# A second buffer for the attention's broadcast target scores, filled eight source tiles before a block's end

## What is computed

```python
x = (meta_x @ W).reshape(N, HEADS, DIM)
a_src = jnp.sum(x * att_src, axis=-1)
a_dst = jnp.sum(x * att_dst, axis=-1)
logits = jax.nn.leaky_relu(a_src[src] + a_dst[dst], NEG_SLOPE)
seg_max = jax.ops.segment_max(logits, dst, num_segments=N)
ex = jnp.exp(logits - seg_max[dst])
alpha = ex / (jax.ops.segment_sum(ex, dst, num_segments=N)[dst] + 1e-16)
out = jax.ops.segment_sum(x[src] * alpha[:, :, None], dst, num_segments=N)
return out.mean(axis=1) + bias
```

## Time and profile before

| | us |
|---|---|
| median of 3 runs (1284.82 to 1287.27) | 1287.16 |
| the profiled execution | 1286.68 |
| its span | 1284.9 |
| counting edges into `C`, to about 408 | 408 |
| hops and the second and third layers, to about 826 | 418 |
| attention, 826 to 1275 | 449 |
| last norm and output | 10 |

### The profile page before, as it was taken

The page is one execution under the profiler, slowest core; times in us unless marked ns, Lnnn a source line. Parts: engine busy times, 40 slices in busy tenths (PEclk is TensorE's granted clock), DMA queues, the critical chain, the costliest instruction groups (busy, mean ns, idle before and its releaser), DMA issues.

```text
span 1284.9 us, 40100 instructions
## 1 busy us (share of the span) xinstructions
PE 1154.3 (90%) x16724; PEld 1074.0 (84%) x16724; DVE 871.6 (68%) x2375; ACT 632.7 (49%) x1161; POOL 62.8 (5%) x113
## 2 busy tenths in 40 slices
PE   0588888888999999999998899599999999999996
PEld 0588888888999999999954899488878888887996
DVE  1899999996443434344642535688878888887887
ACT  0577767661000000000112402578888788788886
POOL 2000000001111111111000002000000000000000
PEclk9866665568999999999999799599999999999998
DMA  1544444420000000000000000000000000000000
GB/s 29 83 71 62 71 61 69 70 51 11 2 3 3 3 3 2 3 3 3 3 2 1 2 3 2 2 2 2 2 2 2 2 2 2 2 2 2 7 12 13
DMA packets 133768, 21.42 MB, mean 17 GB/s; under 512 B 133041, under 2 KB 133458, under 8 KB 133618
## 3 DMA queue, kind: packets, MB, share of 16 engines
q1 hardware_dynamic: 132190, 18.75, 9.7%
q10 hardware_dynamic: 1332, 0.33, 0.1%
q0 software_dynamic: 96, 0.16, 0.0%
HBM read 18.43 MB, written 0.80 MB: 15 GB/s over the span
## 4 chain that ended last, share of the span: by engine, by line
PE 59%; DVE 25%; ACT 7%; issue 6%; DMA 1%; SPq 1%; POOL 0%; DVEq 0%; ACTq 0%; POOLq 0%
PE bank L1786 31%; PE bank L1906 11%; DVE ohk L989 6%; PE bank L1902 6%; ACT Mr L900 4%; DVE ohp L991 4%; DVE Mr L1503 3%; PE bank L1731 3%; DVE raw L979 2%; PE bank L1723 1%; DVE Mr L1510 1%; PE bank L1642 1%; PE bank L1897 1%; DVE oht L949 1%; ACT F L863 1%
## 5 line engine op out<-in xcount | busy, mean ns | idle before, releaser
L1786 PE MATMUL bank<-GH,C 128*128 128x128 f16 x7100 | 397.9, 219 | 0.0
L1786 PEld LDWEIGHTS bank<-GH,C 128*128 128x128 f16 x7100 | 396.9, 98 | 0.1
L1906 PE MATMUL bank<-F,Mr 128*128 128x260 f16 (+1 forms) x2520 | 343.9, 269 | 7.2 <-DVE Mr L1503 3.7
L900 ACT ACTIVATE Mr<-eaT 128x640 f16<-128x640 f32 x433 | 326.5, 822 | 30.0 <-PE bank L1906 28.2
L1906 PEld LDWEIGHTS bank<-F,Mr 128*128 128x128 f16 x2520 | 218.9, 98 | 30.8 <-DVE Mr L1503 4.3
L1503 DVE TENSOR_TENSOR Mr<-Mr,C 128x640 f16<-128x640 f16 x433 | 195.2, 485 | 72.9 <-ACT Mr L900 71.2
L1902 PE MATMUL bank<-FN,C 128*128 128x130 f16 x2260 | 210.0, 220 | 0.8 <-DVE r L1411 0.8
L747 ACT ACTIVATE plo<-bank 128x256 f32<-128x256 f32 (+1 forms) x84 | 30.2, 361 | 362.7 <-PE bank L1786 346.6
L1148 DVE TENSOR_TENSOR S<-bank,plo 128x256 f32<-128x256 f32 (+1 forms) x84 | 33.2, 395 | 210.7 <-ACT plo L747 210.7
L1902 PEld LDWEIGHTS bank<-FN,C 128*128 128x128 f16 x2260 | 164.2, 98 | 10.5 <-DVE r L1411 1.4
L1642 PE MATMUL bank<-ohk,ohp 128*128 128x100 f16 (+3 forms) x1452 | 159.9, 270 | 3.0 <-DVE ohp L991 3.0
(11 more groups left out here) (250 smaller groups left out, 959.6 us busy)
## 6 DMA issues: line engine op xcount, KB each, us to landing
raw<-in_edges_dram SPq DMA_DIRECT2D x242, 68.0 KB, 2.1
xs<-in_x_dram SPq DMA_DIRECT2D x1, 800.0 KB, 4.1
out_dram<-xs SPq DMA_DIRECT2D x4, 160.0 KB
wg<-in_L_gnn_W_dram ACTq DMA_DIRECT2D x2, 64.0 KB
z<-in_L_gnn_att_src_dram SPq DMA_DIRECT2D x1, 128.0 KB, 2.7
z<-in_L_gnn_att_dst_dram SPq DMA_DIRECT2D x1, 128.0 KB, 3.0
out_dram<-xs SPq DMA_DIRECT2D x1, 128.0 KB
wts<-in_L_gnn_W_dram ACTq DMA_DIRECT2D x4, 16.0 KB
```

Of the source, the lines that this page charges most:

```text
L900: act.activation(Mr[:, mi % RB, :], nadS, ACT.Sigmoid, bias=steep[:, h, t:t + 1], scale=-STEEP / XS).then_inc(s_step, 1)
L1786: last = pe.matmul(bank[:, b, jj * 2 * D:(jj + 1) * 2 * D], C[:, t, (t0 + jj) * P:(t0 + jj + 1) * P], GH[:, par, t, :], start=t == 0 and j ...
L1906: return pe.matmul(bank[:, k, a_:z_], Mr[:, mi % RB, j * P:(j + 1) * P], F[:, t, a_:z_], start=start, stop=t == T - 1)
```

## The change

A second buffer for the scores. `wg`, `wa`, `nrm` and `biases`, which were tensors of their own, become parts of one tensor `cold`; its first 640 columns, not needed in the attention any more, are the buffer of odd blocks, and `nadS` becomes a pair indexed by `blk % 2`. The bias that is still needed lies behind column 640.

TensorE writes the next block's scores at t = 17 (`NADS`) and no longer waits for the block's masks; it waits that ScalarE has copied this block's scores (`s_nads`) and that VectorE has read out of the shared bank whatever x.W was put there (`s_vx`, `scaled_by`). ScalarE's copy, which stands behind the block's last sigmoid as before, also waits that the masks of the block before last are done. So that the x.W of a group is read out by t = 17, some steps move: in block 0 of head 0 `xw` from t = 7, 12 to 6, 10, `scaled` from 12, 17 to 10, 15, `high_f` from 13, 18 to 11, 16, `low_f` from 14, 19 to 12, 17; in block 3 the second `scaled` for the next head from t = 18 to 15.

```diff
+    NADS = 17
...
-        wg = sb("wg", [P, H, D], F32)
-        wa = sb("wa", [P, 2, H], F32)
-        biases = sb("biases", [P, 3, D], F32)
-        nrm = sb("nrm", [P, 12, T], F32)
+        cold = sb("cold", [P, GS + H + 12 * T + 3 * D], F32)
...
-        nadS = eaT[:, TP // 2 + VW:TP // 2 + VW + NG * P]
+        nadS = (eaT[:, TP // 2 + VW:TP // 2 + VW + NG * P], cold[:, 0:NG * P])
...
+        def scaled_by(blk):
+
+            h, b = blk // NG, blk % NG
+            return h * NG + (NG if b < NG - 2 else NG + 2 if h < H - 1 and b == NG - 2 else NG + 3 if h < H - 1 else NG)
...
                     act.wait_ge(s_nad, blk + 1)
-                    act.activation(nadS, pnad, ACT.Copy).then_inc(s_nads, 1)
+                    if blk >= 2:
+                        act.wait_ge(s_M, (blk - 1) * T)
+                    act.activation(nadS[blk % 2], pnad, ACT.Copy).then_inc(s_nads, 1)
...
-                            if blk == 0 and t in (1, 6, 13, 18):
-                                high_f(0, (t + 9) // 6)
+                            if blk == 0 and t in (1, 6, 11, 16):
+                                high_f(0, (t + 4) // 5)
...
-                                if t in (5, 12, 17):
-                                    scaled(0, (t + 7) // 6)
-                                elif t in (2, 7, 14, 19):
-                                    low_f(0, (t + 8) // 6 if t > 2 else 1)
+                                if t in (5, 10, 15):
+                                    scaled(0, (t + 5) // 5)
+                                elif t in (2, 7, 12, 17):
+                                    low_f(0, (t + 3) // 5)
...
-                            if b == NG - 2 and h < H - 1 and t in (10, 18):
-                                scaled(h + 1, (t - 10) // 8)
+                            if b == NG - 2 and h < H - 1 and t in (10, 15):
+                                scaled(h + 1, (t - 10) // 5)
...
-                            if blk == 0 and t in (2, 7, 12):
-                                xw(0, 2 + t // 5, blk)
+                            if blk == 0 and t in (2, 6, 10):
+                                xw(0, 2 + t // 4, blk)
...
-                            if t == T - 4 and (h, b) != (H - 1, NG - 1):
-                                pe.wait_ge(s_M, (blk + 1) * T)
+                            if t == NADS and (h, b) != (H - 1, NG - 1):
+                                pe.wait_ge(s_nads, blk + 1)
+                                pe.wait_ge(s_vx, scaled_by(blk))
                                 nad(h + (b + 1) // NG, (b + 1) % NG)
```

More of the change, by code:

```diff
@@ L116, in gnn_kernel @@
         wlrT = wts[:, 5 * D:6 * D]
-        wg = sb("wg", [P, H, D], F32)
-        wa = sb("wa", [P, 2, H], F32)
-        biases = sb("biases", [P, 3, D], F32)
-        nrm = sb("nrm", [P, 12, T], F32)
+        cold = sb("cold", [P, GS + H + 12 * T + 3 * D], F32)
+        wg = cold[:, 0:H * D].rearrange("p (h d) -> p h d", h=H)
+        wa = cold[:, H * D:GS + H].rearrange("p (e h) -> p e h", e=2)
+        nrm = cold[:, GS + H:GS + H + 12 * T].rearrange("p (a t) -> p a t", t=T)
+        biases = cold[:, GS + H + 12 * T:].rearrange("p (a d) -> p a d", d=D)
         starts_row = nrm[0:1].rearrange("p a t -> p (a t)")[:, 0:256].bitcast(I32)
@@ L899, in _ @@
                                         act.wait_ge(s_N, APART[unit_of(mi - RB)] + 1)
-                                act.activation(Mr[:, mi % RB, :], nadS, ACT.Sigmoid, bias=steep[:, h, t:t + 1], scale=-STEEP / XS).then_inc(s_step, 1)
+                                act.activation(Mr[:, mi % RB, :], nadS[blk % 2], ACT.Sigmoid, bias=steep[:, h, t:t + 1], scale=-STEEP / XS).then_inc(s_step, 1)
                 take(H - 1, NG - 1)
@@ L1180, in weights @@
                     c.here()
-                    c.add(v.tensor_reduce(wa[:], att[:], AX, ALU.add))
-                    c.add(v.tensor_tensor(wsq[:, 0:H * D], wg[:].rearrange("p h d -> p (h d)"), wg[:].rearrange("p h d -> p (h d)"), ALU.mult))
+                    c.add(v.tensor_reduce(wa, att[:], AX, ALU.add))
+                    c.add(v.tensor_tensor(wsq[:, 0:H * D], wg.rearrange("p h d -> p (h d)"), wg.rearrange("p h d -> p (h d)"), ALU.mult))
                     c.here()
-                    wa_ = wa[:].rearrange("p e h -> p (e h)")
+                    wa_ = wa.rearrange("p e h -> p (e h)")
                     v.tensor_tensor(wsq[:, H * D:GS + H], wa_, wa_, ALU.mult).then_inc(s_wsq, 1)
                 elif step == 1:
-                    c.add(v.tensor_scalar(w32[:, 0:H * D], wg[:].rearrange("p h d -> p (h d)"), XS, None, ALU.mult))
-                    c.add(v.tensor_scalar(w32[:, H * D:GS + H], wa[:].rearrange("p e h -> p (e h)"), XS, None, ALU.mult))
+                    c.add(v.tensor_scalar(w32[:, 0:H * D], wg.rearrange("p h d -> p (h d)"), XS, None, ALU.mult))
+                    c.add(v.tensor_scalar(w32[:, H * D:GS + H], wa.rearrange("p e h -> p (e h)"), XS, None, ALU.mult))
                     c.here()
@@ L1509, in _ @@
                                         v.wait_ge(s_N, APART[unit_of(mi - RB)] + 1)
-                                v.scalar_tensor_tensor(Mr[:, mi % RB, :], nadS, asad[:, 0, h, t:t + 1], C[:, t, b * NT * P:(b + 1) * NT * P], ALU.is_lt, ALU.mult).then_inc(s_M, 1)
+                                v.scalar_tensor_tensor(Mr[:, mi % RB, :], nadS[blk % 2], asad[:, 0, h, t:t + 1], C[:, t, b * NT * P:(b + 1) * NT * P], ALU.is_lt, ALU.mult).then_inc(s_M, 1)
                             if t and apart(h, b, t - 1):
```

2 lines of the change are left out of this document (1 added, 1 removed).

## The result

The changed kernel takes 1275.14 us (median of 4 runs, 1274.34 to 1275.46), the kernel before 1287.22 beside it (median of 4 runs, 1284.82 to 1294.2): a ratio of 0.9912, interval 0.989 to 0.9935. The ratio is taken over the fast runs and is not the quotient of the two medians (0.9906). The profiled execution has a span of 1273.5 us, against 1284.9. Measured again later it gave 0.9906 (0.9891 to 0.9921).

A forecast was written before the change was run, and what follows sets the result against it. TensorE was taken to pace the attention, so only its standing time could be won: 9.35 + 1.65 - 0.1 + 0.4 = 11.3 us off the median 1287.16 gives 1275.9 us; range 1271.5 to 1281.5, forecast's own bounds 1273.5 to 1279.

The forecast's parts named there:

- What bounds: Attention stage: TensorE, busy 435.5 of 449 us, sets the pace, so only time in which it stands still can be won.
- The removed wait, 9.35 us: Scores' matmuls, blocks 1 to 4 of three heads: TensorE's wait for all masks of the block goes, winning 9.35 us.
- Nothing waits in tiles 18 to 24: Late tiles, tightest in block 4: single masks are ready before TensorE needs them, so all 1.50 us is won there.
- The score matmuls in front of the wait at tile 18, 1.65 us: Block 0 of heads 1 to 3: 0.55 us of score loads before tile 17 fill half the 1.11 us wait, 1.65 us won.
- The new waits at tile 17, 0: Before the early scores: `s_nads` was met a block ago and `s_vx` can never be last, so they cost 0.
- Block 0 of head 0, -0.1 us: Reordered extra work makes tiles 12 and 14 to 17 wait, spending the removed 1.09 us: -0.1 us, between -1.1 and +1.1.
- Starts of blocks, 0.4: Waits hanging on the evictions after tile 24: masks 0 to 2 done earlier win 0.4 us, between 0 and 4.
- ScalarE's copy, cost 0: Score copy (0.70 us) right behind the block's last step: fits in block 4 with 0.1 us to spare, cost 0.
- B: Tight blocks: masks just late in block 4, block 0 of head 0 loses 1 us; gain 5.8, time 1281.4; chance 0.11.
- C: Mask makers' lead also removes waits at block starts and the rest at tile 18: gain 15.8, time 1271.4; chance 0.08.
- D: The wait only moves: TensorE passes the scores and stops as long for masks 17 to 24, 1287 us; chance 0.07.
- E: Mask makers set the pace and VectorE is held before mask 15 in three blocks: slower, 1291.5 us; chance 0.04.

The follow-up runs named there:

- block 0 restored: Changed kernel with VectorE's bias addition early and head 0's block 0 in old step order, scores there at t = 21 without mask wait: 1271.06 us, 0.989.

## Why the prediction was right

By its own steps:

- **What bounds.** TensorE paces the stage: confirmed by head 3, where no period moved by more than 0.2 us in any run, and by doubling ScalarE's copy, which costs 3.4 and not 13 us.
- **The removed wait, 9.35 us.** The periods of blocks 1 to 4 shrank by 3.45 us in each of three heads, 10.35 in all. That is the 9.35 us of gaps between weight loads and about 1.0 for the starts of blocks. By the matmul rows, less block 0's share (0.92), the same term would have been 7.0. The whole stage decides between the two: from the first masked load to the last is 448.5 us before and 436.7 after, 11.9 less. The weight loads' waits for other engines (those over 0.15 us) fell from 19.9 to 8.2, by 11.7, the matmuls' from 15.2 to 5.9, by only 9.4. So the gaps between weight loads were the right ones to take. The Trainium skill (Perfetto Trace Analysis, section Identifying the Most-Contended Engine) calls the matmuls' busy share a poor measure of how close TensorE is to its limit and names the weight loads' busy share, beside another measure, to use instead; of gaps it says nothing. Its reason, that pipelined instructions look smaller in the trace, this trace does not show: in the attention the matmuls are the busier rows (433.4 us against 390.4), and their gaps are the shorter ones.
- **Nothing waits in tiles 18 to 24.** Right: no such row in blocks 1 to 4.
- **The score matmuls in front of the wait at tile 18, 1.65 us.** The waits went from 1.11 to 0.56; the period by 0.52, so 1.56. Putting them back cost exactly that.
- **The new waits at tile 17, 0.** Right: nothing waits at L1906.
- **Block 0 of head 0, -0.1 us.** 28.00 became 28.09. The five waits were 0.4, 0.9, 0.3, 0.8 and 0.3 by the working, 0.38, 0.86, 0.31, 0.79 and 0.29 on the chip. The first of them is partly luck: it is 0.29 in the second profile of the changed kernel, and with the same steps in block 0 it is 0.54 with one buffer and 0.76 with the copy doubled, while from first masked load to first take it stays at 28.09, 28.08 and 27.99 us. One reading in the working is off without an effect on it: the first scaling stands two masks sooner, not three; its time was right.
- **Starts of blocks, 0.4.** Too small: about 1.0. The wait for the eviction after block 4 fell from 0.46 to 0.15 (0.9 over three heads), those at tile 4 of blocks 1 and 2 from 0.36 and 0.39 to 0.32 (0.3), and one at tile 18 of block 4 went (0.2); at tile 11 of block 0 of heads 1 to 3 the wait grew from 0.19 to 0.34 (0.45 back).
- **ScalarE's copy, cost 0.** Right for the time. The sizes around it were off: I expected a wait of about 1.4 us before the takes and found, in head 0, 0.96, 0.47, 0.47, 0.47 and 0.05; only after block 0 of the later heads it is 1.23. I had left out that ScalarE's last sigmoid of a block now waits longer for the ring (a wait of 0.47 us before the change, 1.01 now in block 1), so that part of its slack is used before the copy:

```profile
870.42 0.83 ACT L909 ACTIVATE Mr<-cold,eaT 128x640 f16<-128x640 f32 x1 [1.01 <-PE bank L1915]
871.16 0.68 ACT L885 ACTIVATE eaT<-bank 128x640 f32<-128x640 f32 x1
871.88 2.27 ACT L909 ACTIVATE Mr<-eaT 128x640 f16<-128x640 f32 x3
```

The sum was 11.3 us; the stage gained 11.9, the spans 11.4 and the medians 12.1, whose spread is of the size of these differences. The missing 0.6 are the starts. The bounds given for the forecast, 1273.5 to 1279, are narrower at the low end than its own terms allow: with 4 us at the starts and 1.1 in block 0 it would be 1271.1. Nothing hung on it. Of the rivals, B named the tight place rightly (block 4, where the take follows without idle), but it held. C had the right direction and the wrong size: 0.6 us more than the sum, not 4.5, and the rest of the waits at tile 18 (1.7) stayed. D fell to the changed profile itself, where no wait stands at tiles 18 to 24 of blocks 1 to 4, and E to the run with the moved steps alone and to that with the copy doubled.

## What to carry to other kernels

A wait for a whole batch, put before an instruction that only one late reader conflicts with, charges the pacing engine; let the copying engine wait instead, and give it a second buffer if it has no room for that wait: here the first won 6.5 us and the second 5.4 more, while the buffer without the first won nothing. Read the room of an engine as the idle it has left at the next hand-over after the change, not at the place where it idles now. Work that must be done anyway is free in front of a wait on the pacing engine, and the spacing of extra work on the feeding engines can matter where its sum stays the same (24.94 to 23.23 us a block here); that a lead must be rebuilt between two pieces is the likely reason, not a shown one.

## What the runs showed beyond that

The same instructions ahead of the attention do not take the same time. The kernel with block 0 restored reached its first masked load at 823.31 us in one profile and at 825.97 in the other; over all profiles it came between 823.27 and 826.53. The stage behind it repeats within 0.1 us for the changed kernel.

For this pair the spread arises in the main near the end of the counting and just behind it. ScalarE's 231st copy into `C` starts at 280.6 and 281.1 us, its last one at 290.6 and 292.4, the last product of the hops (`GH` x `C`) at 795.3 and 798.6. The stretch of 280 to 300 us, first profile and second (columns as in the earlier trace rows, the granted clock is the last but two number):

```profile
280.00:300.00 20.00, 13.92 (x236) 13.48 (x234) 15.92 (x50) 9.15 (x20) 0.00 (x0) 0.74 0.19 57
```

```profile
280.00:300.00 20.00, 14.60 (x223) 14.31 (x220) 14.71 (x46) 9.67 (x21) 0.00 (x0) 0.50 0.17 57
```

The granted clock moves between its two levels, 1.2 and 2.4 GHz: in the second profile TensorE had the lower one (0.50) all through this stretch, in the first it had the higher one for about half of it. The kernel before with the second buffer alone, the other early one (823.27), has 0.74 here too, and both profiles of the changed kernel (826.40 and 826.53) have 0.50. Not every stretch at a lower clock costs time: from 100 to 200 us these two have 0.54 and 0.69 and are only 0.13 us apart at the first masked load. What sets the level in these stretches was not tested.

The same is behind the 0.5 us between the two stages of the restored kernel (444.4 and 443.9). In both profiles TensorE stands 2.77 us before the first masked load and then works at 0.50; in the first the granted clock of the fourth microsecond is still 0.50, in the second it is 1.00, and the product x.W before tile 7 comes 8.6 and 7.9 us after the first masked load. The restored block 0 has hardly a wait that could take this up (the 0.20 us at tile 19 gives back a part); in the kernel before and the changed one tile 14 waits for VectorE anyway.

So differences of a microsecond were read from the stage, and not from the span: the 3 us between executions is a quarter of the effect studied here.
